# Bias bands of the third and fourth query tile: stored by ScalarE in the FFN of the batch in front, none by SyncE in self-attention

## What is computed

```python
idx = jnp.clip(pos[None, :] - pos[:, None], -MAX_REL, MAX_REL) + MAX_REL   # MAX_REL = 20
rk2 = rel_k[idx]
rv2 = rel_v[idx]
attn1 = jnp.einsum('bhqd,bhkd->bhqk', q, k)
attn2 = jnp.einsum('bhqd,qkd->bhqk', q, rk2)
attn = jax.nn.softmax((attn1 + attn2) / scale, axis=-1)
w1 = jnp.einsum('bhqk,bhkd->bhqd', attn, v)
w2 = jnp.einsum('bhqk,qkd->bhqd', attn, rv2)
```

## Time and profile before

| what | us |
|---|---|
| median of 3 runs | 2825.82 (2821.31 to 2827.31) |
| profiled execution, its own time | 2818.37 |
| its span | 2815.9 |
| busy: TensorE, VectorE, GpSimd, ScalarE | 2497.2, 1698.8, 1398.6, 1166.3 |
| queue q1 (SyncE) | 371174 packets, 215.76 MB, 30.8% of 16 engines' span |
| queue q10 (ScalarE) | 33024 packets, 5.24 MB, 1.8% |

### The profile page before, as it was taken

One profiled execution on the slowest core, in us unless ns is written; L12 is line 12 of the kernel. 1 busy time (PEld: TensorE's weight loads), 2 busy tenths in 40 slices (PEclk: granted clock), 3 DMA queues, 4 the chain that ended last, 5 costly groups with the idle time before them and its releaser, 6 DMA issues.

```text
span 2815.9 us, 49850 instructions
## 1 busy us (share of the span) xinstructions
PE 2497.2 (89%) x14884; PEld 1712.4 (61%) x14884; DVE 1698.8 (60%) x3890; ACT 1166.3 (41%) x2089; POOL 1398.6 (50%) x1233
## 2 busy tenths in 40 slices
PE   3598899998998989989899889999899898998877
PEld 1366656665676756666566665666567565666645
DVE  4746653786446764477545775368644676447625
ACT  1137423392234732356223742239223473235511
POOL 2457453573445654464543744448344564446432
PEclk8699999999999999999999999999899999999989
DMA  8606200680007600284003820067100770018400
GB/s 248 147 0 161 73 1 8 133 199 27 1 19 169 178 1 1 62 185 120 1 8 87 198 75 1 8 132 194 33 1 14 159 194 1 1 54 184 104 0 8
DMA packets 404494, 224.54 MB, mean 80 GB/s; under 512 B 210590, under 2 KB 400310, under 8 KB 401206
## 3 DMA queue, kind: packets, MB, share of 16 engines
q1 hardware_dynamic: 371174, 215.76, 30.8%
q10 hardware_dynamic: 33024, 5.24, 1.8%
HBM read 129.15 MB, written 91.80 MB: 78 GB/s over the span
## 4 chain that ended last, share of the span: by engine, by line
PE 62%; DVE 12%; issue 9%; ACT 7%; DMA 5%; POOL 3%; SPq 1%; ACTq 0%; DVEq 0%; POOLq 0%
PE PS L1616 56%; PE PS L1619 6%; DMA prob_scr<-arena 3%; ACT arena L1106 2%; DMA arena<-bias_scr 2%; ACT arena L1113 2%; DVE arena L1320 1%; POOL crs L429 1%; DVE arena L1309 1%; DVE PS L1392 1%; DVE cbn L1287 1%; DVE ss L1495 1%; POOL rstd L429 1%; ACT arena L1165 1%; DVE css L1299 1%
## 5 line engine op out<-in xcount | busy, mean ns | idle before, releaser
L1616 PE MATMUL PS<-arena 128*17 128x128 f32 (+7 forms) x6656 | 726.8, 304 | 37.9 <-ACT arena L1106 20.8
L1616 PEld LDWEIGHTS PS<-arena 128*17 128x17 f32 (+2 forms) x6656 | 489.6, 121 | 210.4 <-issue 114.6
L1619 PE MATMUL PS<-ident,arena 128*128 128x128 f32 (+1 forms) x3312 | 507.6, 280 | 89.2 <-DVE arena L447 26.3
L1619 PEld LDWEIGHTS PS<-ident,arena 128*128 128x128 f32 (+1 forms) x3312 | 378.4, 142 | 260.8 <-issue 96.4
L429 POOL TENSOR_TENSOR crn<-crn,mhalf 128x8 f32<-128x8 f32 (+1 forms) x208 | 374.8, 1807 | 163.5 <-DVE crn L1301 162.0
L1616 PE MATMUL PS<-cwk,arena 128*128 128x512 f32 (+1 forms) x832 | 405.9, 611 | 2.5 <-ACT arena L999 2.5
L1392 DVE CUSTOM_DVE_ANT_0 PS<-PS,arena 128x512 f32<-128x512 f32 x512 | 345.5, 710 | 80.1 <-POOL arena L777 52.7
L1106 ACT ACTIVATE arena<-PS,nmax 128x512 f32<-128x512 f32 x512 | 353.4, 726 | 43.0 <-DMA prob_scr<-arena 23.9
L994 ACT ACTIVATE arena<-PS 128x512 f32<-128x512 f32 (+1 forms) x208 | 124.2, 597 | 516.3 <-PE PS L1616 516.3
L1113 ACT ACTIVATE arena<-PS 128x512 f32<-128x512 f32 x384 | 246.0, 642 | 7.3 <-PE PS L1616 5.8
L1616 PEld LDWEIGHTS PS<-cwk,arena 128*128 128x128 f32 (+1 forms) x832 | 156.3, 193 | 127.6 <-issue 114.5
(11 more groups left out here) (162 smaller groups left out, 3801.8 us busy)
## 6 DMA issues: line engine op xcount, KB each, us to landing
arena<-bias_scr SPq DMA_DIRECT2D x128, 336.0 KB, 3.9
prob_scr<-arena SPq DMA_DIRECT2D x128, 336.0 KB, 4.2
q_scr<-arena SPq DMA_DIRECT2D x128, 128.0 KB
arena<-q_scr SPq DMA_DIRECT2D x128, 128.0 KB, 4.2
arena<-k_scr SPq DMA_DIRECT2D x16, 768.0 KB, 12.8
arena<-prob_scr SPq DMA_DIRECT2D x128, 80.0 KB, 3.4
arena<-far_scr SPq DMA_DIRECT2D x16, 546.0 KB, 7.8
arena<-in_ctx SPq DMA_DIRECT2D x16, 512.0 KB, 5.2
```

Of the source, the lines that this page charges most:

```text
L1616: return pe.matmul(o, l, r, start=start, stop=stop, **kw)
L1619: return pe.transpose(o, i, ident[0:i.shape[0], 0:i.shape[0]])
```

## The change

SyncE no longer stores bands in attention. ScalarE stores the band of the third tile after the fourth silu (the copies of its bias values stand before that silu), and that of the fourth after the second `copy_hq`. In the prologue ScalarE stores four bands instead of two. A window's load now waits for one whole store, whatever the tile. SyncE's last waits take in the two other semaphores.

```diff
         def bands_stored(nb, t, g):
 
-            return 16 * (nb + 1) + 1 if t < 2 else 16 * (NG * nb + g + 1) + 1
+            return 16 * (nb + 1) + 1
...
                         elif t:
                             load_band(t - 1, g + NG - 2)
-                        if t < 2:
-                            store_band(sp, b, t + 2, g * HG, (g + 1) * HG)
...
-            for t in range(2):
+            for t in range(T):
                 sp.wait_ge(bias_stored[t], 16 * NB + 1)
...
             act.wait_ge(zeros_stored, 16 * T + 1)
-            for t in range(2):
+            for t in range(T):
                 store_band(act, 0, t)
...
                 silu(3)
                 if not final:
+                    store_band(act, b + 1, 2)
                     copy_r(b + 1, 3)
                 copy_hq(0)
                 copy_hq(1)
+                if not final:
+                    store_band(act, b + 1, 3)
                 copy_hq(2)
                 copy_hq(3)
```

## The result

The changed kernel takes 2848.41 us (median of 5 runs, 2838.01 to 2862.35), the kernel before in the same comparison 2821.31 (2813.8 to 2827.31). The ratio is 1.0097 [1.0057, 1.0137]: slower by 1%, where no change was forecast, and above the range. The profiled execution of the changed kernel is its shortest, 2838.01 us with a span of 2836.2; its span is 20.3 us longer than that of before.

A forecast was written before the change was run, and what follows sets the result against it. TensorE held 62% of the chain of waits; ScalarE bounded the third attention tile. Attention -19.8, FFN window delay +18.2 and prologue +0.5 sum to -1.1 us, from 2825.82 to 2824.7 us; range 2807 to 2843.

The forecast's parts named there:

- Attention loses 8 pieces ... Sum -19.8 us.: Self-attention: without SyncE's band pieces the second tile gains 9.8 us, the first 10; ends -17.5 and -23.4.
- ScalarE's bound plus the third tile's idle time: Second attention tile: ScalarE's busy 130.01 us plus 4.51 idle gives 134.5 instead of 144.3 us.
- The bound of 133.54 from the third tile: First attention tile: at least the third tile's 133.54 us over 8 batches, a gain of 7.7 us.
- I take 3.0 us.: FFN's end: new stores delay each batch's first bias window by 3.0 us, between ends 1.2 and 5.4.
- if the queues take turns packet by packet, as many of the new packets pass, 2560: Before the first window: 2560 new packets pass beside SyncE's query and window packets, costing 2.6 us.
- the rival of the starved window: FFN's end: both stores stand before the first window; sum +16.2, 2842.0 us with 1 us for the prologue; chance 0.18.
- the 16.4 ns of the earlier trace: Price per 160 B packet, from 1899 packets at 32.4% of 16 engines over 6 us; a store takes 2.1 us.
- the high end of 5.4: First window's delay if both new FFN stores, at 2.7 us each, stand in front of it: 5.4 us.
- the second row: Trace from 537 to 539.5: 1905 packets passed alone in 2.5 us, pricing a store at 2.7 us.
- Slack: 0.4 us a batch.: Attention's start: 0.4 us of the window's 3.0 us delay is absorbed; cost 7 x (3.0 - 0.4) = +18.2 us.
- Two more held issues hide. They may still be running when the context is asked for: +0.5 us, ends 0 and 2.: Prologue: ScalarE's idle 27.41 us hides two added issues; transfers overlapping the context loads cost 0.5 us.
- ScalarE held at the first new issue: FFN rival: the store at 542.0 waits up to 6 us for SyncE's descriptor generation; +22.7, 2848.5 us; chance 0.06.

The follow-up runs named there:

- e7: Changed kernel without the new FFN stores (those bands left out from the second batch on), prologue's third and fourth store after the context slots: 2806.74 us, 0.9911.
- e4: Changed kernel with only the third tile's band stored in the FFN, the fourth's by SyncE in four pieces in attention's second tile: 2847.82 us, 1.0077.
- e1: Changed kernel without the two new FFN stores (those bands left out from the second batch on), prologue's four stores kept: 2809.79 us, 0.9937.
- e2: Changed kernel with the prologue's third and fourth store issued after ScalarE's first pass over the context slots: 2852.76 us, 1.0098.
- e3: Changed kernel with both new FFN stores moved behind ScalarE's last FFN copy: 2851.54 us, 1.0091.
- e8: Changed kernel without new prologue and FFN stores; ScalarE stores whole third and fourth bands in attention's first and second tile: 2884.63 us, 1.0199.
- e9: e3 with each new FFN store replaced by 128 packets of 2560 B to a spare buffer: 2819.01 us, 0.9961.
- e5: Changed kernel with each new FFN store replaced by 2048 packets of 512 B (1024 KB) to a spare buffer: 2831.55 us, 1.0016.

## Why the prediction was wrong

**The direction failed: no change was forecast, and it is 1% slower.** Of the 21.4 us between the forecast of -1.1 and the +20.3 of the spans, the way into attention makes 9.8, the prologue 7.9, the end 2.0 and attention 1.6. By the steps of the prediction:

*"Attention loses 8 pieces ... Sum -19.8 us."* About right in size: -18.2 in the tiles of after, -15.9 in those of e7. Wrong in place, so that the size is luck: 6.1 us came from the third and fourth tile, which the sum left out. The second tile gave 15.3 instead of 9.8, since ScalarE's bound plus the third tile's idle time was too cautious: the third tile's idle time itself held the tail of the pieces. With pieces in the second tile the third takes 134.68 us (e4), without them 129.58 (after). The first tile was to give 10 and gave none, and e1 and e7 show that this is not the new stores' doing. The bound of 133.54 from the third tile was the wrong row for it; the first tile also has the start of attention in it, which the prediction named and left at 7.7 us of gain or more.

*"I take 3.0 us."* The place was right: few packets pass beside the keys, and the window lands behind the new ones, 14.5 us after its issue instead of 8.1. The count failed: "if the queues take turns packet by packet, as many of the new packets pass, 2560". The turns held only while the queries ran, and there 2612 new packets passed instead of 2048. Beside the window's own packets nearly all the rest passed, instead of 512: in all 4101 and not 2560, which is the rival of the starved window in full. Why q1 got so few turns after 561 stays open. The price failed too. 4096 packets at the 16.4 ns of the earlier trace rows are 4.2 us, and GpSimd's wait rose by 5.9, above even the high end of 5.4. The 16.4 ns came from a stretch in which the engines were far from full; the second row, by the same measure, has 1.34 x 2.5 x 16 / 1905 = 28 ns. The landing times had it already: a store that stands as 2.1 us of engines in that sum lands after 11.6 us (median of the 16 stores of before), 16.3 in after (of 32).

*"Slack: 0.4 us a batch."* Failed in the other direction. In the batch above 2.3 us of the window's delay were lost in ScalarE's slack, at which the prediction did not look, having read GpSimd's and VectorE's only. Together: 4.0 us a batch reach the first store of probabilities, instead of 2.6: +28 instead of +18.2.

*"Two more held issues hide. They may still be running when the context is asked for: +0.5 us, ends 0 and 2."* The issues hide; the transfers do not. It cost 8.4 us, four times the high end. Of the context loads issued from 101.11 on, the first of 512 KB lands after 13.6 us instead of 4.6, the two behind it after 14.9 instead of 5.4, and e2 and e7 take this back in full at its place. The step failed by the same price: at 2.1 us each, four stores issued from 80.30 on would be done long before 101; in after q10 still moves 925 packets from 103 to 116.

*ScalarE held at the first new issue* fell: 0.37 us in every batch. The second was held 3.0 to 4.5 us, and the copy behind it (557.44) kept its idle time of 3.94 us, as forecast.

*Not in the prediction at all:* the wait at the loop's jump. In after it ends within a microsecond of the window's, so removing either alone returns little in the loop. The eighth batch, outside it, has the window's delay without the jump and lost 7.5 us, more than any other; this is one case. The jump of e3, with the window nearly on time, cost 5.5 to 8.8 us a batch; in after, where the stores come earlier, how much it would cost alone was not separated.

The range's upper end, 2843, took in the starved window but combined it with 1 us for the prologue; the same window with 8.4 is past it. That 2842.0 plus the missing 7.4 is near the measured 2848.41 is luck in part, since the window was charged 35 us there and the way into attention lost 28.

What stays open: why the bands outrun the window from 561 on; why e2's batches are slower than after's; why runs of after spread over 24 us where before has 14; and how wide the gap between profile and medians is to be read, since after's profiled run is its shortest (+20 us in the spans, +27 in the medians).

## What to carry to other kernels

Price a store of many small packets by the count of all its packets, by its landing time and by what else waits on the DMA engines while it drains, not by the engines' busy time for it when it runs alone: moving it to an idle issuing engine frees that engine's queue, not the 16 DMA engines. If the layout allows, fewer and longer packets remove the cost altogether (here, to a spare buffer, 128 instead of 2048); if not, spread them in pieces over a stage whose loads have slack, since a burst cost some 4 us a tile more than pieces (e8). Before moving transfers to the end of a loop's body, look at every engine's first instruction of the next round, also for waits that are marked as issue.

## What the runs showed that was not expected

- With a backlog of small packets an engine's own first instruction behind the jump back of a loop comes late: ScalarE's idle time there is 1.95 us before, 6.17 after, 9.71 in e3, 3.77 in e9; GpSimd's row for it reaches 8.1 us in e3.
- 160 B packets are not a fixed price: with nothing else of note they pass at 762 a us, and from 561 to 564, with a window's load beside them, at 425, while that load passes 132 packets in 3 us. Packets of 512 B, as many of them, cost the kernel half to two thirds as much (e5), although they carry 3.2 times the bytes.
- Two queues with small packets pass them in equal numbers for some 4 us (1343 and 1354), and then no longer (132 and 1274 in 3 us); beside the large key packets a queue of small ones stands still (none in 5 us, then 30 in 3).
- TensorE's mean granted clock is 0.952 in after and 0.959 before. It waits more at the start of each batch; what this costs by itself was not measured.
